# Two layers of attention and feed-forward on one core: score products over a head's own 64 rows, and the router's logits behind the second layer's last unit

## The reference, cut to what matters

```
x: (8, 512, 128)                      # eight sequences, H = 16 heads of D = 8
xn = layernorm(x)
h  = rmsnorm(xn) * norm_w
lin = causal attention with weights (1 + s/2)^2, s = (q Wqf) . (k Wkf), divided by their sum
win = softmax over a window of 64 keys back, causal                   # "slide"
x  = x + (xn + concat(lin, win) @ Wout) + ffn(xn)   # ffn: gate*up, two 512x512 layers with gelu, 512x128
xn = layernorm(x)
x  = x + causal softmax attention(xn) @ Wo + bo     # "causal"
       + mixture of 8 experts, top 2 by logits = xn @ Wg.T
```

## Time and profile before

| | us |
|---|---|
| median of 3 runs | 1279.28 |
| lowest, highest | 1278.79, 1283.72 |
| the profiled execution | 1290.89 |
| its span, first to last instruction | 1289.1 |
| PE busy in the span | 1165.4 (90%) |
| DVE busy | 865.2 (67%) |
| ACT busy | 743.5 (58%) |
| POOL busy | 649.6 (50%) |
| TensorE clock granted, mean | 0.965 of 2.4 GHz |

### The profile page before, as it was taken

How to read it: one execution, slowest core, us unless ns; L and a number is a source line. 1 busy time by engine, 2 the same in 40 slices (tenths; PEclk the granted TensorE clock), 3 DMA queues, 4 the chain that set the end, 5 groups by cost and what they waited for, 6 DMA issues and landing times.

```text
span 1289.1 us, 26679 instructions
## 1 busy us (share of the span) xinstructions
PE 1165.4 (90%) x9122; PEld 750.8 (58%) x9122; DVE 865.2 (67%) x3433; ACT 743.5 (58%) x1580; POOL 649.6 (50%) x846
## 2 busy tenths in 40 slices
PE   5989999999999899989998999899989867988997
PEld 2445754565457545754575457545764456884896
DVE  4066588658865885688658865786578755885563
ACT  2356367735773577457745774477546624557675
POOL 4475254535444454545454544454445436675577
PEclk9998999999999899999999999899989969999999
DMA  7601620162015301540154015401472016542233
GB/s 237 153 3 54 177 73 12 54 184 73 13 55 147 108 15 39 151 120 15 39 152 117 17 39 151 117 17 39 139 211 64 5 26 142 82 70 29 41 55 40
DMA packets 123961, 105.53 MB, mean 82 GB/s; under 512 B 15242, under 2 KB 118578, under 8 KB 123826
## 3 DMA queue, kind: packets, MB, share of 16 engines
q1 hardware_dynamic: 102162, 85.89, 24.7%
q0 software_dynamic: 13792, 9.54, 5.1%
q10 hardware_dynamic: 7872, 8.39, 1.9%
HBM read 58.59 MB, written 46.37 MB: 81 GB/s over the span
## 4 chain that ended last, share of the span: by engine, by line
PE 49%; DVE 21%; ACT 13%; issue 8%; POOL 6%; DMA 2%; DVEq 0%; SPq 0%; POOLq 0%; ACTq 0%
PE bank L700 14%; PE heads L765 11%; ACT probs L1117 8%; PE bank L679 6%; PE bank L707 6%; DVE xnT_s L1585 4%; DVE hrow L1585 4%; DVE hT_s L1585 3%; POOL out L1362 3%; PE bank L690 2%; PE bank L675 2%; DVE spare L1585 2%; PE bank L1050 2%; PE bank L684 1%; PE bank L815 1%
## 5 line engine op out<-in xcount | busy, mean ns | idle before, releaser
L1117 ACT ACTIVATE probs<-bank 128x512 f32<-128x512 f32 (+2 forms) x896 | 441.2, 582 | 176.6 <-PE bank L707 169.8
L1309 POOL TENSOR_SCALAR_AFFINE_SELECT probs<-probs 128x384 f32<-128x384 f32 x256 | 127.7, 521 | 242.1 <-ACT probs L1117 242.1
L765 PE MATMUL heads<-probs,V 128*18 128x192 f32 (+9 forms) x3072 | 194.6, 394 | 10.7 <-POOL probs L1312 4.6
L707 PE MATMUL bank<-K,Q 128*128 128x192 bf16 (+4 forms) x1024 | 199.2, 271 | 4.3 <-ACT probs L1117 0.2
L707 PE MATMUL bank<-Q,K 128*128 128x192 bf16 (+4 forms) x1024 | 175.0, 275 | 16.3 <-ACT probs L1117 7.0
L1362 POOL DMA_INDIRECT out<-h1T_s x78 | 123.2, 1580 | 60.3 <-ACT h1T_s L1270 37.4
L765 PEld LDWEIGHTS heads<-probs,V 128*9 128x9 f32 (+1 forms) x3072 | 78.2, 94 | 122.3 <-issue 85.4
L1262 ACT ACTIVATE h2T_s<-bank,h1T_s 128x128 f32<-128x128 f32 x312 | 89.2, 368 | 93.1 <-PE bank L1050 80.9
L707 PEld LDWEIGHTS bank<-Q,K 128*128 128x128 bf16 x1024 | 81.4, 99 | 87.5 <-ACT probs L1117 31.1
L707 PE MATMUL bank<-QM,K 128*128 128x512 bf16 (+3 forms) x512 | 121.5, 301 | 7.8 <-DVE gatesT_s L1545 1.4
L707 PEld LDWEIGHTS bank<-K,Q 128*128 128x128 bf16 x1024 | 85.2, 98 | 67.7 <-DVE mx_c L1585 14.3
(11 more groups left out here) (241 smaller groups left out, 2285.1 us busy)
## 6 DMA issues: line engine op xcount, KB each, us to landing
K<-slots_of_k SPq DMA_DIRECT2D x64, 256.0 KB, 4.2
Q<-slots_of_q SPq DMA_DIRECT2D x15, 1024.0 KB, 10.9
QM<-slots_of_qm SPq DMA_DIRECT2D x8, 1024.0 KB, 9.4
h1T_s<-sorted_rows SPq DMA_DIRECT2D x78, 65.0 KB
slots_of_q<-Q SPq DMA_DIRECT2D x8, 384.0 KB, 2.6
slots_of_k<-QM SPq DMA_DIRECT2D x8, 384.0 KB, 2.9
slots_of_qm<-Q SPq DMA_DIRECT2D x8, 384.0 KB, 2.6
slots_of_k<-Q SPq DMA_DIRECT2D x8, 384.0 KB
```

The lines of the kernel that those rows point to most:

```text
L707: mm = pe.matmul(to[:, at:at + right.shape[1]], left, right, start=True, stop=True, skip_group_check=True)
L765: mm = pe.matmul(heads[ROWS * i:ROWS * i + n, P * j:P * j + widths[j]], V[:, j, g // 2, i, first:first + n], slot_of(kind, 2 * g + i // 2) ...
L1117: return act.activation(to, bank, func, scale=scale, bias=bias).then_inc(taken_sem(run, unit), 1)
L1309: pool.affine_select(out=three, in_=three, compare_op=ALU.is_ge, fill=0.0, base=0, pattern=[[0, 3], [1, P]], channel_multiplier=-1)
```

## The change

The score products contract over the 64 partitions of their own head (`own(h)`), both operands sliced alike, so that neighbouring products of an even and an odd head stand in different halves of the array's rows. The `_p` units, which put both heads in one bank, keep all 128 partitions. The units of a pair are put into another order: 0a, 1a, 0b, 1b, `_p`, and for `cmax` 1a, 0a, 1b, 0b, `_p`; ACT's and DVE's code follows the same order. In the dense stage the unit `logits` goes behind `h2_3`. The number and the columns of the products stay the same, and no transfer is added or moved.

```diff
+HEADS_OF = {"lin": (0, 1), "causal": (0, 1), "cmax": (1, 0)}
...
 def tri_units(tag):
-    return [f"{tag}{u}" for p in range(H // 2) for u in (f"{2 * p}a", f"{2 * p}b", f"{2 * p + 1}a", f"{2 * p + 1}b", f"_{p}")]
+    return [f"{tag}{u}" for p in range(H // 2) for u in [f"{2 * p + i}{half}" for half in "ab" for i in HEADS_OF[tag]] + [f"_{p}"]]
...
-    units += ["hT2", "k2", "q2", "xnT2", "v2", "logits"] if this else []
+    units += ["hT2", "k2", "q2", "xnT2", "v2"] if this else []
     units += ["h2_3"] if after else []
+    units += ["logits"] if this else []
...
-            def q_part(buf, h, a, n):
-                return buf[:, h // SH, a:a + n]
+            def own(h):
+                return slice(SROWS * (h % SH), SROWS * (h % SH + 1))
+
+            def q_part(buf, h, a, n, of=None):
+                return buf[own(h) if of is None else of, h // SH, a:a + n]
...
-                    parts.append((WQ * (j % 2), q_part(Q1, h, P * j, P), K1[:, h, first:P * (j + 1)]))
+                    parts.append((WQ * (j % 2), q_part(Q1, h, P * j, P), K1[own(h), h, first:P * (j + 1)]))
...
-                def part(h, j, at):
-                    return at, keys[:, h, P * j:P * (j + 1)], q_part(buf, h, P * j, TRI_N[j])
+                def part(h, j, at, of=None):
+                    rows = own(h) if of is None else of
+                    return at, keys[rows, h, P * j:P * (j + 1)], q_part(buf, h, P * j, TRI_N[j], rows)
                 p, u = n // 5, n % 5
-                h = 2 * p + u // 2
+                h = 2 * p + u % 2
                 if u == 4:
-                    parts = [part(2 * p, 2, 0), part(2 * p + 1, 2, 256)]
+                    parts = [part(2 * p, 2, 0, slice(0, P)), part(2 * p + 1, 2, 256, slice(0, P))]
                 else:
-                    parts = [part(h, 1, 0), part(h, 3, 384)] if u % 2 else [part(h, 0, 0)]
+                    parts = [part(h, 1, 0), part(h, 3, 384)] if u // 2 else [part(h, 0, 0)]
...
                 project_rows(run, "v2", hT, wv1[:, :])
+                if after:
+                    dense_low(run, "h2_3", layer2, 3)
                 wait_taken(run, "xnT2")
                 project_rows(run, "logits", xnT, wgT[:, :], E)
-                if after:
-                    dense_low(run, "h2_3", layer2, 3)
-                else:
+                if not after:
                     run_tiles(QUERIED, ROUTED)
```

More of the change, by code:

```diff
@@ L708, in scores_into, with slide_unit @@
                 mm.then_inc(full_sem(run, unit), 1)
-            def q_part(buf, h, a, n):
-                return buf[:, h // SH, a:a + n]
+            def own(h):
+                return slice(SROWS * (h % SH), SROWS * (h % SH + 1))
+            def q_part(buf, h, a, n, of=None):
+                return buf[own(h) if of is None else of, h // SH, a:a + n]
+            def slide_unit(n):
+                half = n % 4 // 2
+                return 2 * (n // 4) + n % 2, (2 * half, 2 * half + 1)
             def slide_max(run, n):
-                h, parts = n // 2, []
-                for j in (2 * (n % 2), 2 * (n % 2) + 1):
+                (h, tiles), parts = slide_unit(n), []
+                for j in tiles:
@@ L723, in causal_max @@
                 p, u = n // 5, n % 5
[L724 removed]
+                h = 2 * p + 1 - u % 2
                 if u == 4:
[L726 removed]
+                    parts = [part(2 * p, 1, 0, slice(0, P)), part(2 * p + 1, 1, 256, slice(0, P))]
                 else:
[L728 removed]
+                    parts = [part(h, 2, 0), part(h, 0, 384)] if u // 2 else [part(h, 3, 0)]
@@ L744, in slide_scores @@
-                for j in (2 * (n % 2), 2 * (n % 2) + 1):
-                    parts.append((WQ * (j % 2), K1[:, h, P * j:P * (j + 1)], q_part(Q1, h, P * j, SLIDE_N[j])))
+                (h, tiles), parts = slide_unit(n), []
+                for j in tiles:
+                    parts.append((WQ * (j % 2), K1[own(h), h, P * j:P * (j + 1)], q_part(Q1, h, P * j, SLIDE_N[j])))
                 scores_into(run, SLIDE_UNITS[n], parts)
@@ L1588, in slide_max @@
             def slide_max(run, n):
-                h = n // 2
+                h, half = 2 * (n // 4) + n % 2, n % 4 // 2
                 def part(j, at):
@@ L1593, in part @@
                     return mx_s[:, to:to + 1], at, slide_neg[:, WIN if j == 0 else 0:WQ]
-                row_max(run, SMAX_UNITS[n], [part(2, 0), part(3, WQ)] if n % 2 else [part(0, 0), part(1, WQ)])
+                row_max(run, SMAX_UNITS[n], [part(2, 0), part(3, WQ)] if half else [part(0, 0), part(1, WQ)])
             def causal_max(run, n):
@@ L1608, in causal_max @@
                 else:
-                    parts = [part(h, 2, 0), part(h, 0, 384)] if u % 2 else [part(h, 3, 0)]
+                    parts = [part(h, 2, 0), part(h, 0, 384)] if u // 2 else [part(h, 3, 0)]
                 row_max(run, CMAX_UNITS[n], parts)
```

14 lines of the change are left out of this document (7 added, 7 removed).

## The result

| | us |
|---|---|
| before, median of 4 (lowest, highest) | 1279.03 (1277.91, 1283.72) |
| after, median of 4 (lowest, highest) | 1295.68 (1293.37, 1296.00) |
| ratio of after to before | 1.0108, 95% interval 1.0088 to 1.0128 |
| profiled execution after, its span | 1295.71, 1294.0 |
| TensorE clock granted, mean, before and after | 0.965, 0.954 |

A forecast was written before the change was run, and what follows sets the result against it. It took DVE to bound the pairs stage, ACT the part behind the gates, and TensorE only 625 to 642 us and the dense stage. Terms -15.8 + 9 + 0 = -7 us took 1279.3 to 1272 us, range 1260 to 1289.

The forecast's parts named there:

- The logits' move: Dense stage: logits behind h2_3 start DVE's first maxima unit 1.4 or 2.9 us earlier a block, 15.8 us in all.
- The third layers: Start of the pairs stage: idling there lowers the clock over half the third layer on average, 1.3 us a block, 9 us.
- The Q2 fetch: Before the first causal maximum: the fetch might become the next limit; nothing taken off, 0 to 0.6 us a block for the range.
- The 64-row products: Scores in pairs and slide stages: overlap of neighbours in different halves and costs of changing rows, taken together as 0.
- I take 0.4 of gain less 0.4 of cost: nothing: The 17 us where TensorE sets the pace: overlap gain and cost of row changes cancel in each block.
- my fourteen changes: The 17 us where TensorE sets the pace: about 14 row changes a block, 0 to 0.15 us each, 0 to 2 us.
- The pairs stage hides its own: Pairs stage, where DVE sets the pace: its changes between 64-row and full-row products cost no time.
- rival B: Rival, 0.14: idling at the pairs start lowers the clock over the whole third layer, lighter scores also between weighs; 1289 us.
- D: Rival, 0.06: changes exposed in the 17 us stretch, +17 us, giving 1289 us; decides from 0.06 us a change.
- A: Rival, 0.12: in the pairs stage faster bank refills halve DVE's gaps behind each weigh, 15 us more gain, 1257 us.
- C: Rival, 0.25: nothing moves; halves don't overlap or changes drain the gain, Q2 or clock take the logits' gain; 1279 us.

The follow-up runs named there:

- the comparison above: The changed kernel against the same with full rows, both run again on one chip: spans 1303.7 and 1279.3 us, 24.4 us more with 64 rows.
- fill64: The changed kernel plus ten unread 512-column products behind the seventh unit of each pairs stage: 1296.18 us, ratio to before 0.9997.
- fill128_again: Full rows, logits behind h2_3 and ten added products in each pairs stage, unchanged from fill128, on another chip: 1276.14 us, ratio to before 0.9835.
- fill128: The kernel before with logits behind h2_3, full rows, plus ten unread 512-column products in each pairs stage: 1272.72 us, ratio 0.9833.

## Why the prediction was wrong

**The logits' move** was right. The wait for xnT_s is gone in all seven blocks. DVE's first unit came 1.56 us earlier in three blocks and 3.12 to 3.19 in four, 17.3 us in all, forecast 15.8. The third layers took 8.9 us more, forecast 9. Alone it gave 4 us where the kernel before takes 1282 and 17.6 where it takes 1298; the forecast was 7. I did not see that this term depends so much on how long the clock stays low behind the old wait, which differs from chip to chip. The Q2 fetch did not come to bind: no wait of TensorE for it stands in the changed kernel's trace. The net gain to the first causal maximum was 7.3 us.

**The 64-row products** are the step that failed: taken at nothing, they cost 17.4 us. "I take 0.4 of gain less 0.4 of cost: nothing" was three errors. (1) I set the cost in the 17 us where TensorE sets the pace at 0.4 us; it was 1.37. Eleven of my fourteen changes cost 0.10 us on the way in and 0.15 on the way out, all exposed, and the three beside a `weigh` cost nothing more. The overlap gave 0.61 us, near the 0.45 in my working. The term was about 0.8 us a block short. (The trace has 98 changes a block, not 79, since my count by units left `weigh` out; that changed nothing.) (2) "The pairs stage hides its own" held for all but 0.39 us a block of some 6 us. That little stands where DVE waits behind a `weigh`. (3) No term held what the 64-row products do to the clock. I had placed the lower clock's price with the logits' move alone, and in rival B as a matter of lighter scores. In the comparison above it cost as much as the changes did: 11 of the 24.4 us, by the second and fourth lines. What of it follows from the longer idling and what from where the blocks happen to fall isn't settled; `fill64` shows the first at the third layer. Nothing shows it at the dense start, where a full-row kernel (`fill128_again`) has 1.2 GHz too in five of six blocks.

**The rivals.** D, the changes exposed, had the mechanism and 0.06 of the chance, at 1289; the measured price of a change, 0.10 us and more, lies over the 0.06 from which it decides. Its working had no share for the clock, though, and took the time against a median at which the forecast's -7 held. B was half right: idling at the pairs stage's start did lower the clock over part of every third layer, but that alone never ate the gain. A failed, since DVE's gaps behind `weigh` stayed. C, nothing moves, lay at 1279.

**The chances.** The nearest row of the old trace was there: 0.21 us of idle weight load at each change between `weigh` and scores. It was the only row on a change, it spoke for a loss, and I set against it a gain for which only rows on column groups stood. Half of that row, 0.10 us, would have been the measured price, and D would have had more than 0.06.

## What to carry over

Count the changes between partial-row and full-row products before you narrow any product: each cost 0.10 to 0.15 us on TensorE here, and a group of four narrow ones between two changes gave back 0.15 us. Whether longer groups pay, no run shows. A single product of 64 rows took as long as one of 128. TensorE's idling of 2.5 to 3.0 us ahead of the third layer was followed by 1.2 GHz over part or all of that layer every time; work without use in that place, 2.2 us a block, made the kernel 4 us faster. And one profile of a kernel whose clock rises and falls is one sample: compare stretches at a full clock, and time both kernels on one chip.

## What was not expected of the hardware

The same kernel took 1282 us on two chips and 1297 on two others, with mean clocks of about 0.97 and 0.96, and a stretch at 2.4 GHz differed by 0.37 us in 81.4. The kernel with less idling ahead of the third layer varied less in two trials: `fill128` took 1272.7 and 1276.1 on two chips where the kernel before takes 1297. And two 64-row products in different halves started 0.003 to 0.014 us apart in the changed kernel, so the halves do run together. In the pairs stage, where DVE sets the pace, no stretch got shorter by it; in the slide stage it gave back less than the changes took.
